# Attention and spectral filter: V projected after the attention, analysis in one matmul per tile and pass

## What is computed

```
# block 1, per image b, c = 128 channels, n = 1024 pixels
hn  = groupnorm16(x) * norm_w + norm_b
q, k, v = wq @ hn + bq, wk @ hn + bk, wv @ hn + bv
att = softmax(q.T @ k * c**-0.5)            # 1024 x 1024
x1  = x + wp @ (v @ att.T) + bp
# block 2
xf     = fftshift(fft2(x1))
center = mean over channels of |xf| at the 7 x 7 middle frequencies
kern   = 7 x 7 kernel made from a small MLP of center     # one per image
filt   = 7 x 7 correlation of xf with kern
out    = ifft2(wr @ filt).real + x1
```

## Time and profile before

| | |
|---|---|
| median of 3 runs | 476.98 us |
| lowest, highest | 476.16, 483.36 us |
| the profiled execution, first to last instruction | 479.0 us |
| TensorE, VectorE busy in it | 428.2, 338.3 us |
| ScalarE, GpSimd busy in it | 246.4, 209.3 us |
| start and image 0, until the loop of images begins | 51.1 us |
| images 1 to 6, each | 43.6 us |
| image 7 and drain, until the analysis ends | 57.7 us |
| last exp of image 0 begins | 50.4 us |
| transfer of gam, 1.49 MB, from issue to landing | 8.8 us |
| TensorE's granted clock | 1.00, but 0.50 from 373 to 407 |

### The profile page before, as it was taken

How to read it: one execution, slowest core, us unless ns; L and a number is a source line. 1 busy time by engine, 2 the same in 40 slices (tenths; PEclk the granted TensorE clock), 3 DMA queues, 4 the chain that set the end, 5 groups by cost and what they waited for, 6 DMA issues and landing times.

```text
span 479.0 us, 7402 instructions
## 1 busy us (share of the span) xinstructions
PE 428.2 (89%) x2535; PEld 365.5 (76%) x2535; DVE 338.3 (71%) x575; ACT 246.4 (51%) x433; POOL 209.3 (44%) x151
## 2 busy tenths in 40 slices
PE   2877898999999999999999999999999159999996
PEld 2655787987798788789878887888889157888884
DVE  3689798579848884984889488758744653766764
ACT  1665565465556555644755565556552502544451
POOL 0463364525434442645254354425512242566552
PEclk9999999999999999999999999999999555987999
DMA  5900000000000000000000000000014000111122
GB/s 184 387 37 0 1 1 0 1 0 0 0 0 0 0 0 0 0 0 0 0 0 0 0 0 0 0 2 0 1 30 99 1 1 0 45 44 44 44 89 88
DMA packets 4799, 13.17 MB, mean 28 GB/s; under 512 B 1488, under 2 KB 2128, under 8 KB 4432
## 3 DMA queue, kind: packets, MB, share of 16 engines
q1 hardware_dynamic: 3488, 12.32, 7.3%
q10 hardware_dynamic: 1296, 0.66, 0.5%
HBM read 8.78 MB, written 4.19 MB: 27 GB/s over the span
## 4 chain that ended last, share of the span: by engine, by line
PE 65%; DVE 21%; issue 6%; ACT 6%; DMA 1%; POOL 1%; DVEq 1%; ACTq 0%
PE PS L355 57%; PE PS L414 6%; DVE ETL L1058 3%; ACT E L784 3%; DVE NMX L1043 3%; DVE GS L972 3%; DVE GS L988 3%; DVE STAT L959 1%; ACT ETH L793 1%; PE PS L440 1%; PE PS L493 1%; DVE VL L1063 1%; DMA X<-in_x 1%; DVE K L1308 1%; DVE XTL L1063 1%
## 5 line engine op out<-in xcount | busy, mean ns | idle before, releaser
L1395 POOL TENSOR_TENSOR E<-E,RI 128x1024 f32<-128x1024 f32 x64 | 122.3, 1910 | 173.9 <-DVE RI L1048 173.8
L784 ACT ACTIVATE E<-PS,NMX 128x1024 f32<-128x1024 f32 x64 | 71.6, 1119 | 50.1 <-DVE NMX L1043 50.1
L793 ACT ACTIVATE ETH<-PS 128x512 fp32r<-128x512 f32 x128 | 69.5, 595 | 46.1 <-PE PS L414 46.1
L1058 DVE TENSOR_TENSOR ETL<-PS,ETH 128x512 fp32r<-128x512 f32 x128 | 81.9, 681 | 7.2 <-ACT ETH L793 7.2
L1043 DVE TENSOR_REDUCE NMX<-PS 128x1 f32<-128x1024 f32 x64 | 78.0, 1219 | 2.8 <-PE PS L355 1.1
L414 PE MATMUL PS<-MISC,E 128*128 128x128 f32 x512 | 67.1, 274 | 5.2 <-DVE ETL L1058 3.2
L414 PEld LDWEIGHTS PS<-MISC,E 128*128 128x128 f32 x512 | 58.7, 140 | 16.6 <-issue 4.7
L355 PE MATMUL PS<-ETH,VH 128*128 128x512 f32 x128 | 55.2, 431 | 0.1
L355 PE MATMUL PS<-ETH,VL 128*128 128x512 f32 x128 | 50.4, 394 | 0.0
L355 PE MATMUL PS<-ETL,VH 128*128 128x512 f32 x128 | 50.0, 391 | 0.0
L1037 DVE SCALAR_TENSOR_TENSOR QL<-PS,BQS,QH 128x512 fp32r<-128x512 f32 x16 | 11.6, 751 | 43.7 <-ACT QH L778 43.7
(11 more groups left out here) (188 smaller groups left out, 880.5 us busy)
## 6 DMA issues: line engine op xcount, KB each, us to landing
X<-in_x SPq DMA_DIRECT2D x7, 512.0 KB, 7.9
out<-X SPq DMA_DIRECT2D x7, 512.0 KB, 2.6
E<-in_gam SPq DMA_DIRECT2D x1, 1488.4 KB, 8.8
SYN<-in_syn SPq DMA_DIRECT2D x1, 1264.0 KB, 12.4
R<-in_ana SPq DMA_DIRECT2D x1, 1138.0 KB, 5.2
X<-in_x ACTq DMA_DIRECT2D x1, 512.0 KB, 4.6
out<-X SPq DMA_DIRECT2D x2, 256.0 KB, 2.0
MISC<-in_misc SPq DMA_DIRECT2D x1, 258.0 KB, 4.2
```

Of the source, the lines that this page charges most:

```text
L784: act.activation(E[:, (t % 4) * N:(t % 4 + 1) * N], s_bank(t), ACT.Exp, bias=NMX[:, t % 2:t % 2 + 1], accum_out=RS[:, t % 4:t % 4 + 1]).th ...
L793: act.activation(et[:, h, 4 * k:4 * k + 4, i * P:(i + 1) * P], bank(ET_BANK + k).rearrange("p (j n) -> p j n", j=4), ACT.Copy).then_inc(s[ ...
L1058: TT(etl[part], bank(ET_BANK + k).rearrange("p (j n) -> p j n", j=4), eth[part].bitcast(F32), ALU.subtract).then_inc(s["v_lo"], 1)
L1395: TT(e, e, RI[:, t % 4:t % 4 + 1].broadcast_to([P, N]), ALU.mult)\
```

## The change

It has these parts.

- V isn't made any more. The V product takes the raw image, transposed: a new input `xt` holds x in 128 x 128 blocks with pixels on partitions, and each image's block is loaded into a tile XTF and split into VH (ScalarE, `value_hi`) and VL (now GpSimd, `value_lo`). Since hn is GA * x + GB per channel and the rows of att sum to one, the sum is scaled by GA after the attention: `out_hi` (ScalarE, with GAO, a copy of GA, as scale) and `out_lo` (VectorE) write it as HNH and HNL. Then `out_project` multiplies by wp @ wv, three matmuls of 512 columns per half, and `residual` adds X and a bias per image, BV, from a one-column product of GB (`group_norm_bias`, read by `bias_of`).
- `in_tile` and `over_tiles` become `features`: 24 matmuls per image, of 302, 330, 358 and 386 columns.
- Group norm has two VectorE operations fewer, and three 128 x 1 tensor_tensors become tensor_scalars with per-partition scalars. The mean's product moves from tile 3 to 4, the variance's from 4 to 5, GA and GB from tile 5 to 6 (behind the row maximum), and hn from tile 7 to tile 6; hn goes to XTF. In image 0 too, hn's low part is now GpSimd's.
- The projections of image b + 1 and the transposes of tile 6 are now at the end of image b, and the analysis of image p stands behind them.
- The synthesis tables are loaded late, into E and XTF (SYF, COSF), when the transposes of image 7's tile 5 are done.

```diff
-                TT(GS[:], GM[:], GM[:], ALU.mult).then_inc(s["v_gn"], 1)
-                TT(GD[:], GS[:], MV[:, 1:2], ALU.add).then_inc(s["v_gn"], 1)
+                TS(GD[:], GM[:], GM[:, 0:1], MV[:, 1:2], ALU.mult, ALU.add)\
+                    .then_inc(s["v_gn"], 1)
...
                 TS(GA[:], GD[:], VEC[:, 0:1], None, ALU.mult).then_inc(s["v_gn"], 1)
-                TT(GS[:], GM[:], MV[:, 0:1], ALU.add).then_inc(s["v_gn"], 1)
-                TT(GS[:], GS[:], GA[:], ALU.mult).then_inc(s["v_gn"], 1)
+                TS(GS[:], GM[:], MV[:, 0:1], GA[:, 0:1], ALU.add, ALU.mult)\
+                    .then_inc(s["v_gn"], 1)
                 TS(GB[:], GS[:], -1.0, VEC[:, 1:2], ALU.mult, ALU.add).then_inc(s["v_gn"], 1)
...
+            def group_norm_bias(n):
+                pe.wait_ge(s["v_gn"], 6 * n + 6)
+                mm(bank(MISC_BANK)[:, GN3_AT:GN3_AT + 1], WVF[:], GB[:], True, True)\
+                    .then_inc(s["p_bv"], 1)
...
+            def out_project(p, h, nxt):
+                pe.wait_ge(s["v_ol"], 2 * p + h + 1)
+                if h == 0:
+                    pe.wait_ge(s["v_bv"], p + 2 if nxt else B)
+                    if is_later(p):
+                        pe.wait_ge(s["a_ur"], p + 1)
+                else:
+                    pe.wait_ge(s["v_xl"], 2 * p + 1)
+                    if nxt:
+                        pe.wait_ge(s["v_bv"], p + 3)
+                d_ = slice(h * HALF, (h + 1) * HALF)
+                for n, (a, r) in enumerate(passes(WH[:, VI, :], WL[:, VI, :],
+                                                  HNH[:, d_], HNL[:, d_])):
+                    ins = mm(bank(MISC_BANK), a, r, n == 0, n == 2)
+                ins.then_inc(s["p_op"], 1)
...
-            def project_v(b, h):
-                for j in range(4):
-                    t0 = (4 * h + j) * P
-                    for n, (a, r) in enumerate(passes(HNH[:, t0:t0 + P], HNL[:, t0:t0 + P],
-                                                      WH[:, VI, :], WL[:, VI, :])):
-                        ins = mm(bank(MISC_BANK)[:, j * P:(j + 1) * P], a, r, n == 0, n == 2)
...
+            def features(t, o):
+                start, width, at = ana_cols(t)
+                cols = slice(start, start + width)
+                for n, (a, r) in enumerate(passes(XTH[:, t, :], XTL[:, t, :],
+                                                  ANH[:, cols], ANL[:, cols])):
+                    ins = pe.matmul(o[:, at:at + width], a, r, start=t == FIRST and n == 0,
+                                    stop=t == LAST and n == 2, skip_group_check=True)
...
+            def out_hi(p, h, pv=PV_BANK):
+                act.wait_ge(s["p_pv"], 2 * p + h + 1)
+                act.activation(HNH[:, h * HALF:(h + 1) * HALF], bank(pv), ACT.Identity,
+                               scale=GAO[:, 0:1]).then_inc(s["a_oh"], 1)
...
+            def out_lo(p, h, pv=PV_BANK):
+                d_ = slice(h * HALF, (h + 1) * HALF)
+                dve.wait_ge(s["a_oh"], 2 * p + h + 1)
+                STT(out=HNL[:, d_], in0=bank(pv), scalar=GAO[:, 0:1],
+                    in1=HNH[:, d_].bitcast(F32), op0=ALU.mult, op1=ALU.subtract)\
+                    .then_inc(s["v_ol"], 1)
...
+            sp.wait_ge(s["p_tr"], 2 * (TILES * B - 2))
+            sp.dma_start(SYF, syn[:, 0:T_COS]).then_inc(s["d_syn"], 16)
+            sp.wait_ge(s["g_vl"], 2 * B)
+            sp.dma_start(COSF[:], syn[:, T_COS:T_END]).then_inc(s["d_syn"], 16)
             sp.wait_ge(s["p_tr"], 2 * TILES * B)
+            sp.wait_ge(s["v_syl"], 2)
             sp.dma_start(E[0:K_ROWS, 0:GAM + NK * NK], gam).then_inc(s["d_gam"], 16)
```

More of the change, by code:

```diff
@@ L52, with ana_cols, pair @@
 UO = CH
-UE = (TILES - 2) * UA
-UI = UE + UB + UA
-UW = UI + UB + UA + UB
+def ana_cols(t):
+    def pair(k):
+        return 2 * UA + UB * (2 * k + 1)
+    own = min(t, TILES - 1 - t)
+    start = sum(pair(k) for k in range(own))
+    width = UA + UB * (own + 1)
+    if t < TILES // 2:
+        return start, width, UO
+    return start + UA + UB * own, width, UO - UB * (own + 1)
+FIRST, LAST = TILES // 2 - 1, TILES - 1
+UW = sum(2 * UA + UB * (2 * k + 1) for k in range(TILES // 2))
+TILE_ORDER = (FIRST, 0, 1, 2, 4, 5, 6, 7)
 HID = 32
@@ L115, in shape_tables @@
     for t in range(TILES):
-        u0 = {0: UE + UB, TILES - 1: UI + UB}.get(t, (t - 1) * UA)
+        start, _, at = ana_cols(t)
+        over = start + UO - at
+        own = start + UA + UB * t if t < TILES // 2 else start
         for hl in range(4):
@@ L475, in analysis @@
                 pe.wait_ge(s["g_al"], 1)
[L476 to L481, removed]
+                for t in TILE_ORDER:
+                    ins = features(t, bank(MISC_BANK))
                 ins.then_inc(s["p_u"], 1)
@@ L1192, in image @@
-                    if prev and t == 6:
-                        misc_lo(XTL[:, 4:8, :], XTH[:, 4:8, :], "a_xh", 2 * p + 2, "v_xl")
+                        row_sum(b, t)
+                    if nxt and t == 2:
+                        stats_end()
+                    if nxt and t == 4:
+                        group_norm_a(b + 1, MISC_BANK)
+                    if nxt and t == 5:
+                        group_norm_b(b + 1, MISC_BANK)
+                    if prev and t == 1:
+                        out_lo(p, 0)
@@ new lines, in image @@
+                    if prev and t == 5:
+                        if not cur:
+                            rt_lo(0)
+                        out_lo(p, 1, pv)
+                    if nxt and t == 6:
+                        hn(b + 1)
+                        bias_of(b + 1)
+                    if prev and t == 6:
+                        residual(p, 1)
+                    if not prev and t == 2:
+                        bias_of(0)
+                    if not prev and t == 3:
+                        dve.wait_ge(s["p_w1s"], 1)
+                        dve.tensor_copy(W1S[:], bank(PV_BANK)[0:NF, W1S_AT:W1S_AT + HID])\
+                            .then_inc(s["v_w1s"], 1)
@@ new lines, in image @@
+                    if t == 2 and not cur:
+                        dve.wait_ge(s["a_sh"], 2)
+                        TT(SYL[:, 0:T_COS], SYF, SYH[:, 0:T_COS].bitcast(F32), ALU.subtract)\
+                            .then_inc(s["v_syl"], 1)
+                        mid = SYH[K_MID:K_LO, T_COS:T_END]
+                        TT(mid, COSF[K_MID:K_LO, :], mid.bitcast(F32),
+                           ALU.subtract).then_inc(s["v_syl"], 1)
+                if prev:
+                    misc_lo(XTL[:, 4:8, :], XTH[:, 4:8, :], "a_xh", 2 * p + 2, "v_xl")
```

415 lines of the change are left out of this document (197 added, 218 removed).

## The result

The changed kernel takes 496.84 us (median of 4 runs, 496.0 to 501.1), the kernel before 476.62 beside it (476.16 to 483.36): ratio 1.044, 95% interval [1.038, 1.050]. The time is inside the predicted range (468 to 502); the likeliest case (481, no change) is not what happened, and slower had 0.36. The profiled execution has a span of 495.7, 16.7 longer than the 479.0 of before; the forecast's sum without the clock was 479.8.

What follows compares the result with a forecast made beforehand. TensorE's work plus waits for short VectorE chains was taken to bound an image; start +1.6, six images -2.4 and end +1.6 on the median 476.98 gave 477.8, and the clock's 3.2 made it 481, range 468 to 502.

Steps and rivals of the forecast that it cites:

- the forecast's sum without the clock: Whole kernel: start 1.6, images -2.4, end 1.6, together +0.8; 479.8 against the profiled span of 479.0.
- TensorE's work: Images 1 to 6: TensorE's matmuls and transposes fall from 41.0 to 38.5 us per image.
- the layout: One image laid out engine by engine, TensorE's work plus waits: period 43.2 us, against 43.60 before.
- Tile 2: V product's next bank waits for out_lo: ready at 9.5, TensorE there at 8.7, +0.9 us per image.
- Tile 6: TensorE waits 1.75 us for GB, then 1.95 for the new bias's read before the second output product.
- Start: Image 0: hn_lo on GpSimd and projections before the loop move its start from 51.1 to 52.7, +1.6 us.
- End: Last image and drain: 59.3 us against 57.7 before, +1.6, with waits for residual, out_lo, XTH and XTL.
- The clock: TensorE's clock falls to half after tile 6 waits, two of six images, 2 us each: +3.2 after hiding.
- rival 1: Group norm's one-column tensor_scalars are held by GpSimd: 46.0 us per image, 496 in all, up to 508; chance 0.31.
- Rival 2: TensorE sets the time, tile 6's chain being shorter than laid out: 456 us, or 467 for half; chance 0.09.
- Rival 3: Start or drain alone is worse, by late tables or a clock fall in the drain: 485 to 488; chance 0.05.
- the analysis' 1.4 per image: Analysis with 24 matmuls in place of 42: 3.8 us for 5.2, saving 1.4 of TensorE's work per image.

Runs made afterwards that it cites:

- fill: Changed kernel with 15 extra 512-column TensorE matmuls in tile 6 of images 1 to 6, around the bias product, filling both waits: 486.6 us, ratio 1.015.
- fill1: Changed kernel with only the 7 extra 512-column matmuls before the bias product, the second wait left empty: 493.0 us, ratio 1.031.
- bvread: Changed kernel with VectorE's read of the new bias moved to right behind GB, ahead of the ETL pair, the reciprocal and hn: 485.5 us.
- experiments 1 to 4: In this order fill, fill1, bvread and experiment 4, all on the changed kernel: 486.6, 493.0, 485.5 and 468.1 us.
- experiment 5: Changed kernel with the old group norm chain, two tensor_tensors each for GD and GS: 515.8 us, ratio 1.075.
- experiment 4: Changed kernel with the bias product and its read moved from tile 6 of the previous image to tile 1 of its own: 468.1 us, ratio 0.974.
- the warm ones: 56 extra matmuls in small-network waits, on before with short norm chain and new analysis (457.6 us), and on experiment 4 with earlier drain residual (457.4 us).

## Why the prediction was right in its range and wrong in its likeliest case

- **TensorE's work, 38.5 per image, and the layout, 43.2: right.** With the waits filled the period is 43.37; 12 x 0.231 and the line through my two analysis rows gave 3.8 for the analysis, the chain of the changed kernel shows 3.80 for its 24 matmuls.
- **Tile 2, +0.9: right in kind**, 0.63 (4.4 us in 7 of TensorE's waits for HNL L1109). **Tile 6, 1.75 and 1.95: right**, 1.54 and 1.89, for the reasons given: GB behind rstd and the maximum, BV's read behind the ETL pair, the reciprocal and hn. hn wasn't held (0.80), and the scaling behind it took 2.39 where 2.7 was laid out.
- **Start, +1.6: too low.** It was +4.2, 55.29 against 52.7. Image 0 has two clock falls of its own, which the sum did not count; in fill, whose profile shows only the first of them, the loop's first V product starts at 53.55.
- **End, +1.6: right**, +1.8. Of its terms the chain shows the wait for the residual, 2.8 for 3.3, the one for out_lo, 1.56 for 1.75, and the one for XTL, 1.41 for 1.6.
- **The clock, +3.2: the step that failed.** The text took "two falls of 2 us" out of a possible six, because the gap was longer than one of 2.26 that had held, but stood between full work. The price was right for a short one, 1.6 each; two of the six were long and cost 2.9. Their number was 6 of 6 in the images, and 2 more in image 0. Six images took 12.9 more than 6 x 43.2: 1.0 is the layout's 0.17 per image, 11.9 the clock (four falls of 1.6 and two of 2.9 make 12.2). With 2.6 from the start and 0.6 from end and rest that is 16.1, where 479.8 and 495.7 lie 15.9 apart. That 496.8 lies inside the range at all is luck: its upper part was made for rival 1, while six falls by the text's own price give 477.8 + 12 = 489.8. The row that I leaned on, a held wait of 2.26, was one event; in the changed kernel a wait of 2.94 in image 0 was followed by a fall, and the same wait, 2.9 to 3.0, in fill, fill1 and bvread was not; waits of 1.5 sometimes are. The Trainium skill ("TensorE: Matmul & The Clock Gate", HAM oscillation — how this bites in real kernels) describes a kernel whose clock falls anew in every tile because TensorE waits for data each time, and asks to restructure so that it stays busy. Here the wait was for VectorE, but the pattern is that one, by the 6 falls of the changed kernel and the 0, 4, 3 and 0 of experiments 1 to 4. No row stood behind two of six: for a wait that comes back alike in every image, one event that held bounds the range, and does not give a middle of it.
- **Rival 1 (one-column tensor_scalars are held): wrong**, though its 496 is the time that came. 0.27 and 0.21 inside GpSimd operations, while the two-input form in the same place is held (experiment 5). The one row for it, a one-source copy of 49x98 held for 1.28, was of more than one column. A time that matches is no proof of its mechanism.
- **Rival 2 (TensorE sets the time): not as the change stands**; moving the bias product (4) makes it nearly so, 40.4 against 38.5 of work.
- **Rival 3 (drain): not here.** The drain took what was laid out, without a fall. That was luck in part: with the same drain, fill and experiment 4 each have a fall in it, for 2.8 and 1.6 us.
- **Credits per part.** The prediction counted the analysis' 1.4 per image in full inside TensorE's work. In the changed kernel's order the chain runs through the analysis, 3.80, without a wait on either side, as laid out, but no run takes it out there; in the old order it gave 0.3. The short chain was worth 2.33 per image on the old kernel and 2.6 on the new, 0.9 of that the clock.

## What to carry to other kernels

A short wait of TensorE that comes back in every pass of a loop can cost itself and then a fall of the clock: here 3.4 us of waits brought 1.6 us more in four passes and 2.9 in two, and waits of 1.5 to 1.9 brought 1.6 in half of the passes or more. Price it so until a run shows it held; the cure was to put the one-column product where its input had long been ready. Before moving a product earlier, ask which VectorE queue its input and its read stand in. Measure each part of a bundled change alone: two operations of one column fewer gave 4% (3% by the loop and the start alone), the analysis under 1% in the old order, and the V projection lost more than both had won until its bias stood elsewhere.

## What was not expected of the hardware

- A one-column tensor_scalar with its scalars from SBUF is not held by a GpSimd operation (0.21 inside one of 1.26), the tensor_tensor GS<-GM,MV is (1.01 in the same), and GM times GM for up to 1.9. The Trainium skill ("GPSIMD Engine Reference", Specifications) names VectorE instructions with two SBUF inputs as contending, and the trace agrees for the tensor_tensor; GS<-GM,MV,GA has three SBUF operands, two of them as scalars, and took 0.27.
- 56 to 90 matmuls whose result nobody reads came with faster kernels: 10 us in fill, where the timeline shows why, and 6 to 7 in the warm ones, where part may be chance.
- Waits of 1.54 + 0.42 us lower the clock in every second image, and one of 1.89 in four of six, though each image runs the same code; the same wait of 2.8 in the drain brought no fall, a short one or a long one in three kernels. What decides it is open.
